# Perceiver block on Trainium2: score and numerator products placed between projection and value products, projection two rounds behind

## What is computed

```python
qkv = (x @ w_qkv).reshape(b, t, 3, H, D)        # b 64, t 32, H 16, D 64; x is layer-normed
q, k, v = (qkv[:, :, 0], qkv[:, :, 1], qkv[:, :, 2])
gate = jax.nn.sigmoid((x @ w_gate).reshape(b, t, H, D))
q = jax.nn.elu(q) + 1.0
k = jax.nn.elu(k) + 1.0
k_cum = jnp.cumsum(k, axis=1)
kv = jnp.cumsum(k[..., None, :] * v[..., :, None], axis=1)
numerator = jnp.einsum('bthj,bthij->bthi', q, kv)
denominator = jnp.einsum('bthj,bthj->bth', q, k_cum)
out = numerator / (denominator[..., None] + 1e-06)
out = out * gate
return out.reshape(b, t, H * D) @ w_out
```

## Time and profile before

| | us |
|---|---|
| median of 3 runs | 961.4 (960.62 to 965.66) |
| the profiled execution | 960.76 |
| its span | 958.9 |
| TensorE busy | 839.8 (88%) |
| VectorE busy | 608.0 (63%) |
| ScalarE busy | 523.9 (55%) |
| GpSimd busy | 237.5 (25%) |

### The profile page before, as it was taken

The page is one execution under the profiler, slowest core; times in us unless marked ns, Lnnn a source line. Parts: engine busy times, 40 slices in busy tenths (PEclk is TensorE's granted clock), DMA queues, the critical chain, the costliest instruction groups (busy, mean ns, idle before and its releaser), DMA issues.

```text
span 958.9 us, 23704 instructions
## 1 busy us (share of the span) xinstructions
PE 839.8 (88%) x9064; PEld 722.7 (75%) x9064; DVE 608.0 (63%) x905; ACT 523.9 (55%) x806; POOL 237.5 (25%) x133
## 2 busy tenths in 40 slices
PE   4889879999999998988757269999999999999994
PEld 3555558888788887878547258898989888888884
DVE  3343432635344361626134839999999999999992
ACT  2433334524343251515102219999998989999981
POOL 1344400000000000000000003555555545555541
PEclk9899979999999998999865559999999999999997
DMA  9799940000000000000834313455545545454542
GB/s 353 255 375 387 386 207 2 3 2 2 2 2 2 1 3 2 2 3 2 325 116 158 106 55 109 126 148 133 141 138 135 140 133 149 125 152 123 158 113 57
DMA packets 34659, 115.81 MB, mean 121 GB/s; under 512 B 4289, under 2 KB 15490, under 8 KB 29474
## 3 DMA queue, kind: packets, MB, share of 16 engines
q1 hardware_dynamic: 27010, 104.35, 31.0%
q0 software_dynamic: 7584, 10.49, 6.1%
HBM read 105.26 MB, written 9.57 MB: 120 GB/s over the span
## 4 chain that ended last, share of the span: by engine, by line
PE 77%; DMA 8%; issue 6%; DVE 5%; ACT 1%; SPq 1%; DVEq 0%; POOLq 0%; ACTq 0%
PE ps L423 18%; PE ps L424 17%; PE ps L425 17%; PE ps L618 6%; DMA ctx_t<-in_ctxT 5%; PE ps L724 3%; PE ps L609 3%; PE ps L589 2%; PE ps L597 1%; PE ps L676 1%; DMA out_x<-y_sb,slot_row 1%; PE ps L480 1%; PE ps L502 1%; PE ps L687 1%; PE ps L661 1%
## 5 line engine op out<-in xcount | busy, mean ns | idle before, releaser
L398 POOL DMA_INDIRECT xs_sb<-xn_d,slot_row x39 | 68.1, 1746 | 513.7 <-DVE slot_row L1260 437.1
L1140 DVE TENSOR_TENSOR w_lo<-w,w_hi 128x1024 fp32r<-128x1024 f32 x156 | 186.9, 1221 | 0.3 <-issue 0.3
L876 ACT ACTIVATE w_hi<-w 128x1024 fp32r x156 | 161.0, 1060 | 7.9 <-DVE tile_e L1221 7.3
L409 POOL DMA_INDIRECT out_x<-y_sb,slot_row x39 | 126.3, 3239 | 118.1 <-ACT y_sb L908 118.1
L423 PE MATMUL ps<-w_hi,xh 128*128 128x512 f32 x312 | 126.8, 406 | 1.3 <-DVE xl L1283 1.3
L425 PE MATMUL ps<-w_hi,xl 128*128 128x512 f32 x312 | 122.6, 393 | 0.0
L424 PE MATMUL ps<-w_lo,xh 128*128 128x512 f32 x312 | 122.3, 392 | 0.0
L423 PE MATMUL ps<-xT_hi,wa_hi 128*128 128x256 f32 x384 | 114.6, 299 | 2.4 <-DVE xT_lo L1055 1.5
L424 PE MATMUL ps<-xT_lo,wa_hi 128*128 128x256 f32 x384 | 110.9, 289 | 0.7 <-issue 0.7
L425 PE MATMUL ps<-xT_hi,wa_lo 128*128 128x256 f32 x384 | 110.8, 288 | 0.0
L887 ACT ACTIVATE w_hi<-w_sb 128x1024 fp32r<-128x1024 f32 x78 | 82.6, 1061 | 28.8 <-DMA w_sb<-in_w 18.5
(11 more groups left out here) (171 smaller groups left out, 1596.1 us busy)
## 6 DMA issues: line engine op xcount, KB each, us to landing
w_sb<-in_w SPq DMA_DIRECT2D x78, 512.0 KB
ctx_t<-in_ctxT SPq DMA_DIRECT2D x16, 1028.0 KB, 7.5
ctx_n<-in_ctxN SPq DMA_DIRECT2D x16, 1024.0 KB
w<-in_w SPq DMA_DIRECT2D x8, 2048.0 KB, 12.0
stage<-in_w_a SPq DMA_DIRECT2D x16, 256.0 KB, 5.8
x_all<-in_x SPq DMA_DIRECT2D x4, 512.0 KB, 7.2
out_x<-x_all SPq DMA_DIRECT2D x1, 2048.0 KB, 7.7
xn_d<-xn SPq DMA_DIRECT2D x4, 512.0 KB, 2.9
```

Of the source, the lines that this page charges most:

```text
L398: pool.indirect_dma_start(xs_sb[:, :], None, xn_d, bass.IndirectOffsetOnAxis(slot_row[:, t:t + 1], 0)).then_inc(f_xs, 16)
L409: pool.indirect_dma_start(out, bass.IndirectOffsetOnAxis(slot_row[:, t:t + 1], 0), y_sb[:, :], None, compute_op=ALU.add).then_inc(f_st, 16)
L876: act.activation(w_hi[:, c, :].rearrange("p (c n) -> p c n", c=DC), w13[:, bass.ds(e, 1), c % 2, :, c // 2 * 512:(c // 2 + 1) * 512].rearr ...
L1140: dve.tensor_tensor(w_lo[:, c, :].rearrange("p (c n) -> p c n", c=DC), w13[:, bass.ds(e, 1), c % 2, :, c // 2 * 512:(c // 2 + 1) * 512].re ...
```

## The change

The projection moves one round further back, to round r - 2, and each of its 16 products stands ahead of 8 of the 128 score products of round r - 1, which move from the end of a step to behind the first two q/k groups of the next. The numerators of round r - 1 are cut in four blocks of 32 products, one behind each value group of round r. The transposes of round r + 1 stand behind the sixth q/k group, with the high part on ScalarE and the low part on VectorE placed to match. `xT_hi`, `xT_lo` and `v_sb` get two buffers each; the step number runs to 9. On VectorE `gated` and `a_lns` move to the start of the step, and `x2` behind the fourth elu. No product, activation or vector operation is added or taken away. The waits of each split function are repeated in each of its calls, and the numerators wait for the low part of the next input besides (`a_lo`), since bank 7 holds both.

```diff
-    xT_hi = place("xT_hi", [P, DC, 2 * P], F32R)
-    xT_lo = place("xT_lo", [P, DC, 2 * P], F32R)
-    v_sb = place("v_sb", [P, 2, HF])
+    xT_hi = place("xT_hi", [P, 2, DC, 2 * P], F32R, "late")
+    xT_lo = place("xT_lo", [P, 2, DC, 2 * P], F32R, "late")
+    v_sb = place("v_sb", [P, 2, 2, HF])
...
-        def a_scores(r):
+        def a_score(r, s, c):
             wait(pe, a_qku, 8 * r + 8)
             wait(pe, a_o, 4 * r)
-            for s in range(2):
-                for c in range(FC):
-                    for b in range(BT):
...
+            for b in range(BT):
...
+        def a_numer(r, u, s, c):
             wait(pe, a_norm, 2 * r + 2)
             wait(pe, a_x2, r)
+            wait(pe, a_lo, min(r + 3, NR))
             wait(pe, a_vu, 4 * r + 4)
...
+        def a_proj(r, u, s, c):
+            wait(pe, a_o, 4 * r + 4)
+            m = pe.matmul(ps[:, 6, s * D:(s + 1) * D], goT[:, u, c, s * P:(s + 1) * P], w_out[:, c, :],
+                          start=c == 0, stop=c == FC - 1)
...
+        def astep(r, u):
+            now, before, older = valid(r, NR), valid(r - 1, NR), valid(r - 2, NR)
+            if now:
+                wait(pe, a_lo, r + 1)
+                a_qks(r, u, range(0, 2))
             for s in range(2):
                 for c in range(FC):
+                    if older:
+                        a_proj(r - 2, u, s, c)
+                    if before:
+                        a_score(r - 1, s, c)
             if now:
-                wait(pe, a_lo, r + 1)
-                a_qks(r, range(0, 2))
+                a_qks(r, u, range(2, 4))
             if before:
                 a_dens(r - 1)
             if now:
-                a_qks(r, range(2, 8))
-                a_gates(r)
-            if before:
-                a_nums(r - 1)
+                a_qks(r, u, range(4, 6))
+            a_trs(r + 1)
             if now:
-                a_values(r)
-            a_trs(r + 1)
-            if before:
-                a_proj(r - 1, 1 - u)
-            if now:
-                a_scores(r)
+                a_qks(r, u, range(6, 8))
+                a_gates(r, u)
+            for n in range(4):
+                if now:
+                    a_values(r, u, n)
+                if before:
+                    for c in range(n % 2 * FC // 2, (n % 2 + 1) * FC // 2):
+                        a_numer(r - 1, 1 - u, n // 2, c)
...
# VectorE
         def astep(r, u):
-            before = valid(r - 1, NR)
+            before, older = valid(r - 1, NR), valid(r - 2, NR)
+            if older:
+                gated(r - 2, u)
+            a_lns(r + 1)
             if before:
                 masks(r - 1)
-            elu(r, 0)
-            elu(r, 1)
+            for n in range(4):
+                elu(r, n)
+            if older:
+                x2(r - 2)
             recip(r - 1, 0)
-            elu(r, 2)
+            elu(r, 4)
             recip(r - 1, 1)
-            elu(r, 3)
-            elu(r, 4)
+            elu(r, 5)
             recip(r - 1, 2)
-            elu(r, 5)
+            a_lo_ev(r + 1, 1 - u)
             elu(r, 6)
             recip(r - 1, 3)
             elu(r, 7)
```

More of the change, by code:

```diff
@@ L186, in build @@
     xn2 = place("xn2", [P, 2, D], where="late")
-    assert at["late"] <= TOP_ADDR - 2 * DC * 4 * HF * 4
     qT = place("qT", [P, FC, 2 * P])
     kT = place("kT", [P, FC, 2 * P])
-    xT_hi = place("xT_hi", [P, DC, 2 * P], F32R)
-    xT_lo = place("xT_lo", [P, DC, 2 * P], F32R)
-    v_sb = place("v_sb", [P, 2, HF])
+    xT_hi = place("xT_hi", [P, 2, DC, 2 * P], F32R, "late")
+    xT_lo = place("xT_lo", [P, 2, DC, 2 * P], F32R, "late")
+    v_sb = place("v_sb", [P, 2, 2, HF])
     goT = place("goT", [P, 2, FC, 2 * P])
+    assert at["late"] <= TOP_ADDR - 2 * DC * 4 * HF * 4
     assert at["low"] <= W13_AT, (at, W13_AT)
@@ L541, in a_trs @@
             wait(pe, a_ln, 2 * r + 2)
-            wait(pe, a_o, 4 * r - 4)
+            wait(pe, a_o, 4 * (r - 2))
             for dc in range(DC):
@@ L547, in a_trs, with across @@
             m.then_inc(a_tr, 1)
-        def across(bank, f):
+        def across(u, bank, f):
             for half in range(2):
@@ L562, in a_qks, with a_gates @@
                     wait(pe, a_qku, 8 * r + n - 3)
-                across(n % 4, (n % 2) * HF + (n // 2) * 2 * P).then_inc(a_qk, 1)
-        def a_gates(r):
+                across(u, n % 4, (n % 2) * HF + (n // 2) * 2 * P).then_inc(a_qk, 1)
+        def a_gates(r, u):
             for n in range(4):
                 wait(pe, a_qku, 8 * r + n + 5)
[L568 to L578, removed]
@@ L580, in a_scores, with a_values @@
-        def a_scores(r):
+                across(u, n, 3 * HF + n * 2 * P).then_inc(a_gt, 1)
+        def a_values(r, u, n):
+            s, j = n // 2, n % 2
+            wait(pe, a_gtu, 4 * r + n + 1)
+            f = 2 * HF + j * 512
+            for dc in range(DC):
+                m = mm3(ps[:, n, :], xT_hi[:, u, dc, s * P:(s + 1) * P], xT_lo[:, u, dc, s * P:(s + 1) * P],
+                        wa_hi[:, dc, f:f + 512], wa_lo[:, dc, f:f + 512], dc == 0, dc == DC - 1)
+            m.then_inc(a_v, 1)
@@ L592, in a_scores @@
-            m.then_inc(a_sc, 1)
+            for b in range(BT):
+                tok = slice(s * P + b * T, s * P + (b + 1) * T)
+                for h in range(2):
+                    rows = slice(h * HD, (h + 1) * HD)
+                    m = pe.matmul(ps[b * T:(b + 1) * T, 4 + h, (s * FC + c) * T:(s * FC + c + 1) * T],
+                                  kT[rows, c, tok], qT[rows, c, tok], start=True, stop=True,
+                                  tile_position=(h * HD, b * T))
+            if s == 1 and c == FC - 1:
+                m.then_inc(a_sc, 1)
@@ L598, in a_dens @@
                           start=True, stop=True).then_inc(a_den, 1)
-        def a_nums(r):
+        def a_numer(r, u, s, c):
             wait(pe, a_norm, 2 * r + 2)
             wait(pe, a_x2, r)
+            wait(pe, a_lo, min(r + 3, NR))
             wait(pe, a_vu, 4 * r + 4)
+            for h in range(2):
+                for b in range(BT):
+                    rows = slice(b * T, (b + 1) * T)
+                    m = pe.matmul(ps[h * HD:(h + 1) * HD, 4 + b, (2 * c + s) * T:(2 * c + s + 1) * T],
+                                  v_sb[rows, u, s, (2 * c + h) * HD:(2 * c + h + 1) * HD], att[rows, s, c, h, :],
+                                  start=True, stop=True, tile_position=(b * T, h * HD))
+            if s == 1 and c == FC - 1:
+                m.then_inc(a_num, 1)
@@ new lines, in a_proj @@
+        def a_proj(r, u, s, c):
+            wait(pe, a_o, 4 * r + 4)
+            m = pe.matmul(ps[:, 6, s * D:(s + 1) * D], goT[:, u, c, s * P:(s + 1) * P], w_out[:, c, :],
+                          start=c == 0, stop=c == FC - 1)
+            if s == 1 and c == FC - 1:
+                m.then_inc(a_y, 1)
+        def astep(r, u):
[3 more added lines that the diff above has]
+                a_qks(r, u, range(0, 2))
@@ L644, in _ @@
         pe.wait_ge(l_wo, 32)
-        for r in range(NR + 1):
+        for r in range(NR + 2):
             astep(r, r % 2)
@@ L811, in _, with a_hi_ev @@
         NR = NT // 2
-        def a_hi_ev(r):
+        def a_hi_ev(r, u):
             if not valid(r, NR):
@@ L816, in a_hi_ev @@
             wait(act, a_tr, r + 1)
-            wait(act, a_v, 4 * r)
-            act.activation(xT_hi[:, :, :], ps[:, 7, :].rearrange("p (c d) -> p c d", c=DC), ACT.Copy).then_inc(a_hi, 1)
+            wait(act, a_v, 4 * (r - 1))
+            act.activation(xT_hi[:, u, :, :], ps[:, 7, :].rearrange("p (c d) -> p c d", c=DC), ACT.Copy).then_inc(a_hi, 1)
         def elu_parts(r, ns):
@@ L836, in astep @@
             if now:
-                elu_parts(r, range(0, 2))
+                elu_parts(r, range(0, 4))
             if before:
@@ L840, in astep @@
             if now:
-                elu_parts(r, range(2, 8))
+                elu_parts(r, range(4, 6))
+            a_hi_ev(r + 1, 1 - u)
+            if now:
+                elu_parts(r, range(6, 8))
                 for n in range(4):
@@ L849, in astep @@
                     wait(act, a_v, 4 * r + n + 1)
[L850 to L855, removed]
+                    wait(act, a_num, r - 1)
+                    act.activation(v_sb[:, u, s, j * 512:(j + 1) * 512], ps[:, n, :], ACT.Copy).then_inc(a_vu, 1)
+        a_hi_ev(0, 0)
+        for r in range(NR + 2):
             astep(r, r % 2)
@@ L1049, in a_lns, with a_lo_ev @@
                 normed(xn2[:, s, :], 2 * r + s, 1, a_ln)
-        def a_lo_ev(r):
+        def a_lo_ev(r, u):
             if not valid(r, NR):
@@ L1116, in astep @@
                 norm_att(r - 1)
[L1117 to L1123, removed]
+            if older:
+                wait(dve, a_x2, r - 1)
                 for s in range(2):
-                    stats_of(2 * (r - 1) + s, 2, a_bn)
+                    stats_of(2 * (r - 2) + s, 2, a_bn)
         dve.wait_ge(s_split_lo, NPIECE)
@@ L1129, in _ @@
         a_lns(0)
```

(4 more changed lines are left out.)

6 lines of the change are left out of this document (3 added, 3 removed).

## The result

The changed kernel takes 973.6 us (median of 4 runs, 969.95 to 980.98) against 961.0 for the kernel before (4 runs); the ratio is 1.014, with a 95% interval of 1.007 to 1.021. I had forecast 959 in a range of 940 to 983, with slower by over 0.5% at 0.36. The time lies in the range, but the forecast, a small gain, had the wrong sign.

What follows compares the result with a forecast made beforehand. TensorE was taken as the bound, losing time to instruction-supply stalls and a lowered clock. From 960.8 us, -28.3 - 16 + 37.4 + 3.5 + 2.7 - 1 = -1.7 gave 959.0 us, range 940 to 983.

Steps and rivals of the forecast that it cites:

- Gain 1, supply: Loop's small products: breaking runs ends "issue" stalls from instruction supply; 28.3 us gained, 2 left in for numerator blocks, bounds 15-32.
- 53 records a us: Supply rate taken from a stalled run of 256 small records in 4.8 us; numerator blocks ask for 29.
- Gain 2, clock: Gated-attention loop, 141 to 466 us: without stalls the clock has no cause to fall; 16 us gained, bounds 0-18.
- Switches: TensorE changing between whole-array and small products: 0.29 us per score pair, 0.33 per numerator pair; 37.4 us cost.
- A: Rival on TensorE's changes: switches are cheaper in the mix, 0.19 us a pair; 944 us, chance 0.22.
- B: Rival on TensorE's changes: each drains more, 0.45 us a pair by modelled record ends; 979 us, chance 0.12.
- "Costed at nothing", the waits: Extra waits in split calls on values reached long before: cost nothing; bounds 0 and 3 us, 0.1 per 28 numerator blocks.
- Step 8 (2.7 us for the gated product): Start of step 8: no q/k group covers the gated product there, costing 2.7 us.
- Rival D: Mixed projection and score stretch: the clock falls to 1.2 GHz, 48 us more; 1007 us, chance 0.04.
- VectorE (3.5): Last gate group: TensorE waits for VectorE's last elu, 0.5 us booked a round; 3.5 us cost, bounds 0-10.
- C: Rival on numerator blocks: supply can't refill between them, one stall and clock drop a round; 978 us, chance 0.13.
- E: Rival on the loop: VectorE becomes the bound by 1.4 us more a round; 969 us, chance 0.07.

Runs made afterwards that it cites:

- The scores twice over: Kernel before with every run of scores issued twice, 512 records in a run instead of 256: 1032.4 us in one run, loop 411.8.
- the last experiments: Changed kernel with waits once a round, xT in its old place, numerators in two blocks; projection and scores in groups of 1, 8, 16: loops 332.2, 308.4, 328.1 us.
- one by one: Against the groups-of-eight kernel, projection and scores alternate singly in six steps, 16 pairs of switches instead of two: 953.4 us, 0.992 of the kernel before.
- groups of eight: Changed kernel with waits once a round, step 8 unmixed, old xT place, eight projection products per group, numerators in two blocks: 930.3 us, 0.970 of the kernel before.
- step 8 apart: Changed kernel with, in step 8 alone, all 16 projection products and then all 128 scores: 969.8 us, 1.010 of the kernel before.

## Why the prediction was wrong

My terms, applied to the loop, give 337.9 - 28.3 - 16 + 37.4 + 3.5 + 2.7 = 337.2 us. It was 351.0.

- **Gain 1, supply (28.3 forecast): right, if anything short.** "Issue" before small products fell from 30.2 to 2.4 us. The two microseconds kept for the numerator blocks were 0.5. The scores twice over and the count by 256 show the cause. One reading was too high: 53 records a us is not what the supply can do in a longer run, it is 128 in 3.7 us, 35. The numerator blocks ask for 29, which is nearer to it than I thought, and the one stall that came stood there.
- **Gain 2, clock (16): right** up to step 8: 0.94 became 0.99 over 325 us.
- **Switches (37.4): right.** A piece of the mix is 0.85 us, 0.31 ahead of the scores and 0.12 behind them, as in the earlier trace rows; a pair costs 0.28 in the trace and 0.283 in the loops of the last experiments (0.29 forecast). Rivals A and B, at 0.19 and 0.45, are both out. The Trainium skill (TensorEngine Tiling, Key Properties) says that a change of tiling mode drains TensorE. The runs agree in so far as every pair of changes costs its 0.28 us; whether that is a drain they don't show, and it wasn't the modelled ends of the records that TensorE waited for (that would be 0.45).
- **"Costed at nothing", the waits: this step failed.** I had bounded the repeated waits by 0.1 us for each of 28 blocks, on the ground that small products behind them are queued while dense ones stream. Four waits are two instructions of 51 ns on TensorE's queue in every call, and a block with them took 1.18 us instead of 0.86. Issued once a round they cost the loop 9.2 us less (10.2 less 0.2 in step 8 and 0.8 of a supply stall), of the 13.8 that were missing. The first round's blocks of 0.87, with one wait fewer, were the hint in the changed kernel; in the kernel before, there was no row of a wait in the middle of a run of small products, and "no row shows it" was no bound.
- **Step 8 (2.7 us for the gated product): mis-sized.** The idle time was there, 2.63 us. But the clock fell with it, and I had charged the mix that follows at full clock: 20.4 us from first projection to last score instead of 13.4 (my expectations have 13.0, which is too low), 7.0 more in the profiled execution. In another trace with the same instructions in step 8 it was 2.4 more. Rival D had the mix and the low clock together, at the wrong place: the mix doesn't lower the clock in the six steps that it enters at 2.4 GHz. Whether it makes a low clock last longer isn't shown.
- **Placing xT: not seen.** 0.0024 us on each of some 1100 products would be 2.7 us; putting it back took 1.7 off outside step 8.
- **VectorE (3.5): too dear.** TensorE waited for the last elu six times for 1.3 us in total, an estimated 2.5 if each wait also exposes the 0.2 us that I had taken for the stalls.

9.2 + 7.0 + 1.7 is 17.9; less 1.5 for supply, 1 for VectorE and 1 for the switches it is 14.4, against the 13.8 that were missing (351.0 - 337.2). The waits are more than half of it, and the part of step 8 is of this one execution. Rivals C and E didn't come: no supply stalls a round, no VectorE bound.

That the kernel is slower is so by side costs, and by the waits first: without them alone the ratio is 1.002 (0.999 to 1.005). The order of the change is not the trouble, nor is the idea of breaking the runs: without the side costs and with the numerators in two blocks it wins 0.8% one by one, where the switches take most of what it wins, and 3% in groups of eight, which are as long as a block of instructions.

## What to carry to other kernels

When a long run of small products stalls on "issue", break it with dense work, but in pieces as long as the instruction supply allows, since every pair of changes of kind (to small products and back) costs TensorE a fixed 0.28 us here: count the pairs. A function that is split into many calls must not repeat its waits in each; one in the first call holds for all. And idle time costs twice: the clock fell with each of the 2.6 us waits ahead of step 8, and what followed ran at half speed for 3.4 us or more, so look for a way to fill the idle time itself. Whether dense products behind it bring the clock back sooner is a question that these runs leave open.

## What the runs showed of the hardware

- In a run of small fp32 products TensorE does 128 records (with their weight loads) in 1.1 to 1.3 us, then idles for 2.0 to 2.5: one block of 256 instructions each 3.7 us. All 82 stalls stand at the same place of a block, by count. While expert weights were being loaded (DMA share 1.0) a stall was mostly 4.4 to 5.3 us, but 1.9 with step 8 apart in the changed kernel (DMA share 0.96).
- Of separate wait instructions, already satisfied, the first in each call of 16 small records costs up to 0.02 us, and each further one 0.07 to 0.1 us (0.3 to 0.4 for a block of four calls). Behind a dense product one costs nothing that shows: each of 96 score calls had one as well, and the mixed stretch is 13.5 us with them and without.
- The clock fell at or soon after 2.6 us of idle time ahead of step 8, in all ten traces that have it. With 32 projection records behind it the low level lasted 3.4 or 6.8 us, with pieces of two projection and 16 score records 3.4 to 17.1 us. The same pieces, entered at 2.4 GHz, stayed there in all six other steps.
- The moving operand's place in SBUF moved the distance of 256-column fp32r products from 0.1172 to 0.1197 us, and back to 0.1176.
